# A two-layer transformer on one core: a new order of the steps, bias rows loaded first, V columns centred piece by piece

## What is computed

```python
q, k, v, g = x@w_q+b_q, x@w_k+b_k, x@w_v+b_v, x@w_g+b_g        # layer 0, 1024 rows x 256
sim = einsum(rot(q), rot(k)/scale) * decay_mask ; ret = sim @ v
ret = (ret - mean) / sqrt(var + eps) * gn_weight + gn_bias      # per head
x = ln(x + (silu(g)*ret) @ w_o + b_o)
x = ln(x + (sigmoid(x@Q(w1).T) * (x@Q(w2).T)) @ Q(w3).T)        # Q: round to -1, 0, 1
x = ln(x + softmax(causal(q k^T / 4)) v @ Wo + bo)              # layer 1
x = ln(x + shared(x)*sigmoid(x@W_sgate) + top2_experts(x))
```

## Time and profile before

| | |
|---|---|
| median of 3 runs | 453.7 us (452.33 to 457.52) |
| the profiled execution | 457.42 us, of which the span from first to last instruction 455.7 us |
| TensorE / VectorE / ScalarE / GpSimd busy | 81% / 67% / 49% / 39% |
| mean granted TensorE clock | 0.899 of 2.4 GHz |

### The profile page before, as it was taken

The page is one execution under the profiler, slowest core; times in us unless marked ns, Lnnn a source line. Parts: engine busy times, 40 slices in busy tenths (PEclk is TensorE's granted clock), DMA queues, the critical chain, the costliest instruction groups (busy, mean ns, idle before and its releaser), DMA issues.

```text
span 455.7 us, 8248 instructions
## 1 busy us (share of the span) xinstructions
PE 369.2 (81%) x2700; PEld 210.6 (46%) x2700; DVE 307.5 (67%) x807; ACT 221.5 (49%) x460; POOL 176.5 (39%) x216
## 2 busy tenths in 40 slices
PE   0987977889788889888886878787889899999990
PEld 0455655564455534344364433233566545555560
DVE  4666388535578785475479896853888787858635
ACT  4697435344425413787881136766333434545510
POOL 3276486243612002541320003583124552438544
PEclk9989797557979967998989788999999999999997
DMA  7999993011001000044110000013211214153151
GB/s 237 354 252 237 234 239 127 26 41 47 1 0 48 1 0 2 0 115 140 47 47 1 1 1 2 34 61 98 58 28 44 74 68 105 60 145 136 60 163 46
DMA packets 25853, 38.53 MB, mean 85 GB/s; under 512 B 2130, under 2 KB 21138, under 8 KB 25810
## 3 DMA queue, kind: packets, MB, share of 16 engines
q1 hardware_dynamic: 23060, 31.41, 25.7%
q0 software_dynamic: 2208, 6.07, 3.7%
q10 hardware_dynamic: 544, 0.52, 0.4%
HBM read 30.88 MB, written 17.49 MB: 106 GB/s over the span
## 4 chain that ended last, share of the span: by engine, by line
PE 52%; DVE 22%; ACT 9%; issue 7%; POOL 5%; DMA 3%; SPq 1%; POOLq 0%; DVEq 0%; ACTq 0%
PE psum_a L614 8%; DVE arena_mixers L1338 6%; PE psum_a L892 6%; PE psum_a L751 5%; PE psum_a L906 5%; PE psum_a L861 4%; PE psum_b L614 3%; PE psum_b L823 3%; DVE cut_weights L1163 2%; ACT arena_mixers L1059 2%; PE psum_a L797 1%; POOL arena_mixers L1522 1%; PE psum_b L763 1%; PE psum_a L674 1%; DVE ln_stats L1152 1%
## 5 line engine op out<-in xcount | busy, mean ns | idle before, releaser
L1551 POOL TENSOR_TENSOR ln_rstd<-ln_var_eps,minus_half 128x1 f32<-128x1 f32 x32 | 20.8, 649 | 86.0 <-DVE ln_var_eps L1154 85.9
L614 PE MATMUL psum_a<-cut_weights,x_transposed 128*128 128x512 f16 (+1 forms) x198 | 41.0, 364 | 12.6 <-DVE cut_weights L1163 11.7
L1338 DVE TENSOR_REDUCE arena_mixers<-psum_a 128x2 f16<-128x768 f32 (+3 forms) x44 | 47.3, 1126 | 4.3 <-PE psum_a L797 4.2
L1059 ACT ACTIVATE arena_mixers<-psum_a 128x1024 f32<-128x1024 f32 (+2 forms) x48 | 40.5, 884 | 7.5 <-PE psum_a L813 7.3
L1540 POOL DMA_INDIRECT expert_out<-block_out,arena_ffn x30 | 29.3, 976 | 31.2 <-ACT block_out L1110 25.6
L1568 POOL TENSOR_SCALAR_AFFINE_SELECT arena_mixers<-arena_mixers 128x256 f32<-128x256 f32 (+1 forms) x48 | 24.5, 516 | 41.7 <-ACT arena_mixers L1059 41.4
L892 PE MATMUL psum_a<-cut_weights,stage 128*128 x180 | 32.1, 314 | 7.4 <-issue 3.4
L614 PEld LDWEIGHTS psum_a<-cut_weights,x_transposed 128*128 128x128 f16 x198 | 20.6, 109 | 29.0 <-DVE cut_weights L1163 11.6
L861 PE MATMUL psum_a<-x_transposed,cut_weights 128*128 128x512 f16 (+1 forms) x144 | 33.0, 380 | 0.7 <-ACT arena_mixers L1059 0.7
L1556 POOL TENSOR_TENSOR arena_ffn<-arena_ffn 128x512 f16<-128x512 f32 (+1 forms) x12 | 13.8, 1160 | 48.7 <-ACT arena_ffn L1029 48.7
L1163 DVE SCALAR_TENSOR_TENSOR cut_weights<-stage,cut_weights 128x1024 f16<-128x1024 f32 (+3 forms) x21 | 24.1, 1169 | 6.6 <-ACT cut_weights L927 6.5
(11 more groups left out here) (252 smaller groups left out, 852.6 us busy)
## 6 DMA issues: line engine op xcount, KB each, us to landing
expert_in<-in_row_init SPq DMA_DIRECT2D x1, 10140.0 KB, 52.6
stage<-in_wexp SPq DMA_DIRECT2D x9, 512.0 KB, 3.6
arena_ffn<-expert_in SPq DMA_DIRECT2D x30, 130.0 KB, 2.1
stage<-in_wsh SPq DMA_DIRECT2D x5, 437.0 KB, 10.7
arena_mixers<-expert_out SPq DMA_DIRECT2D x6, 256.0 KB, 3.9
arena_ffn<-in_w SPq DMA_DIRECT2D x1, 1408.0 KB, 7.5
stage<-in_xT SPq DMA_DIRECT2D x2, 512.0 KB, 4.3
stage<-in_wqkvg SPq DMA_DIRECT2D x2, 512.0 KB, 5.3
```

The lines of the kernel that those rows point to most:

```text
L614: ins = mm(dst, lhs[k][a], rhs(k, b, col), start=(k == 0 and a == 0 and b == 0), stop=(bias_at is None and k == n - 1 and a == 1))
L1059: ins = nc.scalar.activation(heads, by_row_tile(ps, se_heads(j))[:, :, :, 0:w], ACT.Exp, scale=1.0 / 16)
L1338: v.tensor_reduce(ST[:, i, 0, h0:h0 + n_h, 48].rearrange("p (h s) -> p s h", s=2), by_row_tile(ps, n_h)[:, :, :, 0:(i + 1) * P], AX.X, ALU ...
```

## The change

- The bias rows are loaded first, already doubled to two rows in memory, with the factor for their rest (0 and 64) in one more column; so the bias's rest does not need the constants any more.
- `cen 0` is new: it centres the bias row alone. `cen 1` and `cen 2` stand behind the split of the piece before, and centre one piece each. The list begins `cen split bias cen split cen split split`.
- ScalarE makes the heads of the columns of q, k (512) and gate (256) of pieces 1 and 2 without waiting for the centring, and only the head of the V columns (256) behind it. That is three copies instead of one for each of the two pieces.
- `ORDER` is written anew, with other PSUM tiles. It holds the same steps and `cen 0`.
- A word may end in `+n`, for n filling products ahead of the step (`FILLS`, `fill`); no word of the new list does.

```diff
 ORDER = """
-    split cen cen split split bias split split proj:a0 rot pg:a2 pg:a1 tqk:b1 proj:a2 wsum proj:a1 split split sc:a0
-    sc:a1 split wsum kv:b0 rot rot proj:a2 ret:b0 tqk:a1 vr:a0 proj:a1 tqk:b1 sc:a2 sc:a1 kv:b1 kv:a2 rx:a1 wsum
-    sc:a2 rot rot yg tqk:b0 yh ret:b1 sc:a1 sc:a0 vr:a1 wo0:a2 proj:a1 ln0 gsum:a0 rx:b1 yg ret:b0 sc:a1 tqk:b0
-    vr:a1 quant quant proj:a0 tx0:b0 sc:a1 ret:b1 yh vr:b0 quant rx:b0 yg rot proj:a0 kv:b1 rx:b0 tqk:a0 wo0:a1 bias
-    yh sc:a0 sc:a1 rot sc:a0 kv:b0 split ret:b1 yg ret:a0 wo0:b0 yh vr:b0 kv:a2 ln0 wo0:a1 tx0:a1 rot split ln0
+    cen split bias cen split cen split split proj:a1 rot split pg:a0 pg:a2 proj:a1 tqk:b1 wsum proj:a1 split split
+    split sc:a1 sc:a2 wsum rot kv:b0 proj:a0 ret:b0 tqk:b1 rot vr:a0 proj:a1 tqk:b1 sc:a0 sc:a2 rx:b0 kv:b1 kv:b0
+    wsum sc:a2 rot yg tqk:a1 yh ret:b0 sc:a0 sc:a1 rot vr:b1 wo0:b1 gsum:a1 proj:a2 quant ln0 rx:b1 sc:a1 tqk:a0
+    ret:b0 sc:a0 vr:b0 yg quant proj:a1 tx0:a0 yh ret:b1 vr:a2 quant rx:b0 yg rot proj:a0 rx:b1 yg kv:a1 tqk:a0
+    rot kv:b1 yh sc:a0 sc:a1 sc:a0 wo0:a2 split tqk:a0 ret:a2 wo0:b0 bias yh vr:b1 ln0 wo0:b0 rot kv:a0
...
-    yh tx1:a0 ln1 yg dn:b1 dn:a1 ln1 tx1:b0 ln0 ln0 yh tx1:a1 split wo0:a0 tx0:b1 wo0:b0 ln1 qk:a2 ln0 ln0 tx0:b1
-    qk:a1 tx1:b0 tq:a2 qk:a0 mx:a2 qk:a0 tq:a1 tq:a2 mx:a0 mx:a1 mx:a2 tq:a0 mx:a2 mx:a1 tm:a0 mx:a2 mx:a0 mx:a2
+    yg dn:b1 ln1 yh ret:a0 vr:b1 dn:b0 dn:b1 ln1 rx:b1 yg ln1 tx1:b0 yh tx1:a1 dn:a2 tx1:a1 ln0 ln1 wo0:a0
+    wo0:b0 qk:a2 tx1:b0 ln0 ln0 qk:a1 split qk:a0 tq:a2 tq:a1 tx0:b1 qk:a0 mx:a2 tq:a0 mx:a2 mx:a1 mx:a0
...
-    se:a0 pv:b0 sh sh su:a1 se:a2 pv se:a0 bx:b1 bx:a1 bx:a2 bu:a0 bx:b1 sh bi pv pv bu:a2 ya:b1 bi su:a1 ty:b0
+    se:a0 se:a1 su:a2 su:a1 pv:b0 se:a2 pv se:a0 bx:b1 bx:a1 sh bx:a2 bi bi pv pv ya:b1 ya:b0 su:a1 bu:a0 sh
...
-    fin ln3 ln3 sd:b1 sd:b0 sd:b1 sd:b0 os os os fin fin os ln3 fin ln3 fin ln3 ln3
+    bd:a2 bt:b0 bd:a0 bt:b1 bd:a2 bd:a1 fin ln3 sd:a0 sd:a2 sd:b1 sd:a0 os os fin os fin os ln3 fin ln3 fin ln3
+    ln3
 """
+    add(("cen", 0))
         if i in (1, 2):
-            add(("cen", i), at(i > 1, ("cen", 1)))
+            add(("cen", i), ("split", i - 1))
-    add(("bias", 0), ("cen", 2))
+    add(("bias", 0), ("cen", 0))
-        bias_raw = cut([8 * D])
+        bias_raw = cut([8 * D + 1])
@@ SP
+            sp.dma_start(bias_raw[0:2, :], bias_rows).then_inc(bias_in, 16)
             load(0)
             load(1)
-            sp.dma_start(bias_raw[0:2, :], bias_rows.partition_broadcast(2)).then_inc(bias_in, 16)
             load(2)
@@ TensorE
+                if step in FILLS:
+                    claim(step)
+                    fill(ps if len(ps.shape) == 2 else ps[:, 0, :], FILLS[step])
@@ ScalarE, split
+                    dst, src = split_views(i, 0)
                     if i in (1, 2):
-                        act.wait_ge(v_centred, i)
-                    dst, src = split_views(i, 0)
+                        for w in (slice(0, 2 * D), slice(3 * D, 4 * D)):
+                            nc.scalar.activation(dst[:, w], src[:, w], ACT.Copy, scale=SW)
+                        act.wait_ge(v_centred, i + 1)
+                        dst, src = dst[:, 2 * D:3 * D], src[:, 2 * D:3 * D]
                     nc.scalar.activation(dst, src, ACT.Copy, scale=SA if name == "xT" else SW).then_inc(head_cut, 1)
@@ VectorE, cen and bias
+            def centre(rows, w, total):
+                heads = w.rearrange("p (h d) -> p h d", h=RH)
+                link(v.tensor_reduce(total, heads, AX.X, ALU.add))
+                link(v.tensor_scalar(total, total, -1.0 / RD, None, ALU.mult))
+                v.tensor_tensor(heads, heads, total.unsqueeze(2).to_broadcast([rows, RH, RD]), ALU.add).then_inc(v_centred, 1)
+                    if i == 0:
                         dve.wait_ge(bias_in, 16)
+                        centre(2, bias_raw[0:2, 2 * D:3 * D], v_sum[0:2, 2])
+                    else:
+                        dve.wait_ge(piece_in[i], 16)
+                        centre(P, stage[:, i % NSTAGE, 2 * D:3 * D], v_sum[:, i - 1])
                 elif kind == "bias":
-                    if n == 1:
-                        dve.wait_ge(con_in, 16)
                     dve.wait_ge(bias_head, n)
-                    v.scalar_tensor_tensor(bias[0:2, w], bias_raw[0:2, w], con[0:2, C_REST:C_REST + 1], bias[0:2, w],
+                    v.scalar_tensor_tensor(bias[0:2, w], bias_raw[0:2, w], bias_raw[0:2, 8 * D:8 * D + 1], bias[0:2, w],
```

More of the change, by code:

```diff
@@ new lines @@
+    se:a2 up:a0 se:a1 pv:b0 cut se:a0 se:a2 dn:b1 ln1 pv se:a2 pv se:a0 se:a2 pv tx1:b1 pv:b0 split dn:b1
+    split split se:a2 se:a1 se:a0 ln1 dn:b1 split ln1 qk:a0 pv se:a1 tx1:a2 tx1:b1 split pv se:a1 pv se:a0
+    split qk:a2 qk:a1 se:a2 se:a0 dn:b1 pv:b0 se:a2 pv se:a0 ln1 tx1:b1 pv split se:a0 se:a2 qk:a1 split pv
+    pv:b1 se:a2 se:a0 se:a1 pv split pv split split se:a1 tq:a2 tq:a0 pv mx:a1 ya:b0 ya:b1 mx:a1 ty:b0 ty:b1
+    tq:a0 mx:a1 tq:a2 ya:b0 mx:a0 mx:a1 mx:a0 wo2:a2 ty:a1 ya:b1 wo2:b0 tm:a2 mx:a0 mx:a2 tm:b1 mx:a1
@@ L140, in at @@
         return step if condition else None
+    add(("cen", 0))
     for i, (name, _, _, first) in enumerate(PIECES):
         if i in (1, 2):
-            add(("cen", i), at(i > 1, ("cen", 1)))
-        add(("split", i), at(i, ("split", i - 1)), at(i in (1, 2), ("cen", i)), ("qk", NB - 1, TB - 1) if name == "wexp" and first < EARLY else None)
-    add(("bias", 0), ("cen", 2))
+            add(("cen", i), ("split", i - 1))
+        add(("split", i), at(i, ("split", i - 1)), at(i == 0, ("cen", 0)), at(i in (1, 2), ("cen", i)), ("qk", NB - 1, TB - 1) if name == "wexp" and first < EARLY else None)
+    add(("bias", 0), ("cen", 0))
     add(("bias", 1), ("bias", 0), ("split", 4))
@@ L232, in pv_at @@
     return ("pv", n // (AH // 4 * TB), n // TB % (AH // 4), n % TB)
+FILLS = {}
 def schedule():
+    FILLS.clear()
     need = dependences()
@@ L243, in schedule @@
     for word in ORDER.split():
+        word, _, fills = word.partition("+")
         key, _, tile = word.partition(":")
@@ L247, in schedule @@
         order[step] = True
+        if fills:
+            FILLS[step] = int(fills)
         if tile:
@@ L625, in x_tiles, with fill @@
                 return [[XT[:, a, k, t * P:(t + 1) * P] for a in range(2)] for k in range(KD)]
+            def fill(dst, times):
+                pe.wait_ge(con16_in, 16)
+                for _ in range(times):
+                    mm(dst[:, 0:2 * P], ident16, con16[:, 0:2 * P], start=True, stop=True)
             offset = {}
```

57 lines of the change are left out of this document (20 added, 37 removed).

## The result

| | before | after |
|---|---|---|
| median, device us | 455.61 (452.33 to 459.84, 4 runs) | 440.09 (436.48 to 441.49, 4 runs) |
| ratio, 95% interval | | 0.967, 0.957 to 0.977 |
| span of the profiled execution | 455.7 us | 434.7 us |
| TensorE busy / idle in that span | 369.2 / 86.5 us | 348.4 / 86.3 us |
| time at the lower clock level, 2 x (1 - mean clock) x span | 92 us | 42 us |

The change made the kernel 15.5 us faster at the median (3.3% by the ratio), where 450.7 us was predicted and 444 to 461 was the range. Executions over 1.5% above the fastest of the same kernel count in the medians of this document, but not in its ratios. The table says where to look: TensorE's idle time did not move by a microsecond, and yet the span is 21.0 us shorter, nearly all of it in busy time (20.8 us), with the same 2700 products.

What follows compares the result with a forecast made beforehand. No engine was full (TensorE busiest, 81%), so waits in single stretches decided. Terms 0.6 - 2.7 + 0.6 - 1 - 0.5 = -3.0 took the profiled 457.4 to 454.4, at the median's ratio 450.7 us; range 444 to 461.

Steps and rivals of the forecast that it cites:

- the last sentence of the prediction: Whole kernel: the forecast would be wrong if the 92 us of half-clock time were redistributed by more than 10 us.
- Rival 2: Retention stage: the clock stays up without the two waits, 5.5 us more than the sum, 445.3 us; chance 0.27.
- Rival 3: First batch's attention, about 190 to 240 us: clock half for 20 us more, costing 10, 460.7 us; chance 0.19.
- Its sign: The granted clock between 190 and 240 us was to show whether the slower case had come.
- The start, +0.6: Kernel start: first product at 11.6 us as before, then a wait of 0.6 after six products; costs 0.6 us.
- The selects, -2.7: Retention stage: causal selects go ahead of a GpSimd power, removing waits of 1.77 and 0.97; saves 2.7 us.
- The held powers, 0: GpSimd powers beside VectorE's quantising: a third held power would be covered by a projection; 0, bound +1.4 us.
- The first row maximum, +0.6: Attention stage: the first row maximum moves behind a 2.27 us wait for ScalarE; costs 0.6 us, bounds 0 and +1.2.
- the tiles, -1: PSUM tiles: new assignment shortens TensorE's waits for copies out; saves 1 us, bounds 0 and -4.
- The expert start, -0.5: Expert blocks: the 1.06 wait before the first up product is hidden, the gathered-block wait stays; saves 0.5 us.
- The end, 0: Kernel end: VectorE's list from the last shared product on is the same, GpSimd's powers early enough; 0 us.

Runs made afterwards that it cites:

- x1: The kernel before with only the head of its order list new (bias rows first, centring per piece, V heads apart): 456.16 us, ratio 1.001.
- x4: x1 with 55 products nobody reads put into nine TensorE waits between 62 and 103 us, no step moved: 446.21 us, ratio 0.981.
- x14: x1 with products nobody reads in four TensorE waits of the middle stretch (119 to 143 us): 451.97 us, ratio 0.996.
- x9: x1 with steps 109 to 202 (first feed-forward to the first batch's row maxima) in the new order and tiles: 447.23 us, ratio 0.987.
- x11: The changed kernel up to the end of the second batch's row maxima (313 steps), the old order from there on: 434.53 us, ratio 0.958.
- x10: The changed kernel with one output projection and its GpSimd power put back ahead of the fifth tile's scores: 443.23 us, ratio 0.977.
- x8: x1 with one output projection and its GpSimd power moved behind the sixth tile's scores: 450.19 us, executions too far apart for a ratio.
- x13: x1 with 12 and 7 products nobody reads in the two waits for the selects (76 and 79 us): 451.33 us, ratio 0.995.
- x5: The changed kernel with the copy of the block indices moved ahead of the shared expert's third product: 439.97 us, ratio 0.961.
- x6: The changed kernel with 24 products nobody reads in TensorE's wait for the first gathered expert rows: 439.74 us, ratio 0.962.

## Why the prediction was wrong, step by step

Lengths of the stretches in the profiled executions, us, with the time at the lower level in brackets (from the clock's records in the trace):

| | before | x1 | x4 | x14 | x9 | after | x11 |
|---|---|---|---|---|---|---|---|
| start to `proj 7` | 65.9 (10.2) | 67.0 (10.2) | 66.3 (3.4) | 65.1 (3.4) | 66.8 (10.2) | 63.9 (3.4) | 65.7 (6.8) |
| `proj 7` to `up 0 0` | 38.3 (30.5) | 38.4 (30.8) | 30.5 (0) | 38.4 (30.7) | 37.9 (30.1) | 29.6 (3.4) | 29.8 (6.8) |
| `up 0 0` to `qk 0 0` | 32.2 (10.4) | 32.0 (10.2) | 28.5 (0) | 30.2 (3.4) | 28.8 (4.0) | 26.8 (0) | 26.8 (0) |
| `qk 0 0` to `tm 0 3` | 49.6 (13.7) | 50.0 (13.7) | 48.5 (10.2) | 46.3 (0) | 44.6 (0) | 44.2 (0) | 44.2 (0) |
| `tm 0 3` to `tm 1 3` | 83.8 (17.1) | 81.6 (10.0) | 82.3 (13.7) | 82.2 (13.7) | 82.4 (13.7) | 81.3 (16.9) | 81.3 (16.9) |
| `tm 1 3` to `sd 7` | 172.3 (3.4) | 171.8 (3.7) | 172.9 (3.4) | 172.4 (3.4) | 172.2 (3.4) | 175.4 (10.4) | 170.3 (0.2) |

**The step that failed** is the last sentence of the prediction: the sum has no term for the redistribution of the half-clock time. In rows two to four the old list without half clock takes 30.5, 28.5 and 46.3 us (x4, x4, x14) against 120.4 in x1: the clock is worth 7.9 + 3.5 + 3.7 = 15.1 us in these traces. The new list takes 29.6, 26.8 and 44.2: shorter waits are worth about 0.9 + 1.7 + 2.1 = 4.7 there (a little more, as `after` still has 3.4 us at the lower level; a little less, as the filling products may hold the old list up). The first stage is 3.1 us shorter with 6.8 us less at the lower level, and the last gives back 3.6. A rough price from one kernel's own executions: the ten of x9 run from 446.34 us at a mean clock of 0.931 to 452.56 at 0.913, that is 6.2 us for 17 us more at the lower level, 0.36 us each. From before to after 50 us of it went; that is 18 us at that price, for 21.0 in the span. The medians say the same more fairly: the 19 executions of before beside x1 have 86 us at the lower level on average and the four of the changed kernel 52. These 34 us make about 12 of the 15.5 us measured, and what is left, about 3, is the size of the prediction's own sum. If the price holds, the waits were about right in sum, and the missing term was four times as large.

Rival 2 named this ("the clock stays up in the retention stage", 445.3), and failed twice in size: it took half of 10.9 us where the runs show 7.9 for that stretch, and it looked at that stretch alone. The half clock at 125 to 132 and 162 to 176 us stood in the same trace and had no rival; it was worth as much again (7.2). Rival 3, half clock in 190 to 240 us of the old trace's time, did not come: the changed kernel has 3.4 us of it in the same steps, where the old one had 6.8. Its sign, the clock between 190 and 240 us, misleads as it stands: it is 0.89 there in the changed kernel, since the kernel is some 20 us ahead and the half clock of the second batch's row maxima (232.3 to 246.0) falls into the window.

**The start, +0.6**: right in its mechanism (first product 12.06 for 11.6, wait 0.54 for 0.6, gate products 17.21 for 16.5), and x1 has +0.5 us against before, inside its interval of -1.5 to +2.5. The gate products came 0.7 later than told, and 0.4 of that is one operation: L1162 took 0.81 instead of 0.42.

**The selects, -2.7**: the wait went, as it said. By x4 to after the whole stretch is worth 0.9 us, 2.2 if the 3.4 us at the lower level are taken off at 0.36; waits of 1.39 and 1.94 took the place. The wait was also not the order's alone: it stood behind a power of 2.53 us, and in x10, where the power is ahead of the selects again but takes 0.56, TensorE has no wait for these selects. What it missed is what the waits did to the clock: x8 moves one step and gains 6 us at the median, x13 fills the waits and gains 4.8 with the selects as late as before.

**The held powers, 0**: right. One of the eight powers was held (2.87 us, at 64.1), where before there were two (3.01 at 58.9 and 2.87 at 65.9); a third did not come.

**The first row maximum, +0.6, and the tiles, -1**: the row maximum stands behind the wait at 132.86 as told, and the waits of the kind in the earlier trace rows fell from 9.9 in 16 to 7.9 in 13. Together the two terms are -0.4; x9 against x14 and x4 shows -1.7 in that stretch, and the one ahead of it takes 28.8 us with 4.0 at the lower level against 28.5 with none. The sign of the sum was right and the size within its bound of -4.

**The expert start, -0.5**: wrong. The step was "the wait for the gathered block stays: the row sends on GpSimd have the same steps ahead of them". The gather waits for two things, and the prediction followed one. The table (`rb 0`) was put behind `su 0 2` and one of its operations, L1426, took 3.23 us while GpSimd's selects and L1553 ran; in x5 and in the kernel before it took 0.28. The Trainium skill, SBUF — State Buffer, section "Who interferes with whom", has the rule for this, a VectorE operation with two SBUF inputs and a GpSimd operation that reads SBUF shut each other out, and the trace agrees. Exchanging this part (x11) is worth 5.6 us: the 10 us at half clock behind the wait make about 3.7 of that by the rough price. Neither moving the table (x5) nor filling the wait (x6) gained by itself, and the trace of x5 is slowed by a half clock that has nothing to do with the step; how the 5.6 us divide stays open.

**The end, 0**: right, from `bd 29` to `sd 7` 7.4 us in every run.

What stays open: why one wait is followed by a long fall and another is not. The stretches ahead of the fall at 77.0 before, and ahead of that at 78.7 after:

```profile
66.00:77.00 11.00, 8.72 (x63) 5.93 (x60) 9.34 (x21) 5.50 (x10) 8.05 (x6) 0.84 0.56 169
```

```profile
64.00:78.70 14.70, 10.10 (x92) 7.04 (x89) 12.73 (x28) 7.30 (x15) 8.38 (x8) 1.00 0.83 217
```

TensorE worked 8.72 of 11 us and the clock then fell for 30.7 us; it worked a smaller part, 10.10 of 14.7, and the clock fell for 3.4 us. The sum of waits ahead does not tell the two apart. The Trainium skill, TensorE: Matmul & The Clock Gate, section "A second HAM failure mode: psum-queue depth-cycling", says that short idles between groups of products can make the clock swing between its levels. The traces agree in kind: behind the first product no idle of TensorE is over 4.5 us, nearly all are under 2, and up to the last product the clock falls eleven times before and five times after.

## What to carry to other kernels

Before the waits are added up, list the stretches at the lower clock with their lengths, and give each a price from products of one kind at both levels. A change of order that moves a few waits of 1 to 2 us is a bet on those stretches first and on the waits second, and both signs of that bet belong in the range. Compare the mean clocks of several executions before one trace is explained: the profiled one may be the best or the worst draw, as with the changed kernel and x5 here. If only the clock is in doubt, fill the waits of the unchanged kernel with products that nobody reads: what is gained is the least that the clock was worth, and it says nothing on whether fills pay in a list that runs at full clock anyway. And where a step waits for several producers, follow each one through both orders.
